# f and g of the conv attention: projected channel-major in fp32 with 32-row fp32 scores, instead of a bf16 stack built on GpSimd

## The chip, the core and the metric

The kernel runs on one core of one Trainium2 chip. The metric is the device time of one execution in microseconds (us); the smaller the better. TensorE (PE) multiplies matrices into PSUM, VectorE (DVE) and ScalarE (ACT) read PSUM and SBUF, GpSimd (POOL) works in SBUF, and SyncE (SP) issues the DMA transfers. Each engine runs its own instructions in program order, and they wait for each other on semaphores.

## The reference

Eight images (batches) of 256 tokens with 128 channels go through three blocks. The change touches the first.

```python
xf = x.reshape(b, n, c)                              # 8 x 256 x 128
f, g, hh = xf @ Wf + bf, xf @ Wg + bg, xf @ Wh + bh  # 16 columns each
attn = softmax(einsum('bnd,bmd->bnm', f, g))         # 256 x 256 scores per batch
x = gamma * (attn @ hh) @ Wv + bv + xf               # "conv" block
t = x + attention_block(ln(x))     # 8 heads of 16, softmax, W_comb, layernorm, cos, FFN of 512, layernorm
out = t + moe(ln(t))               # 32 experts, the top 2 weighted, all computed densely
```

## The kernel before

A batch of 256 tokens is two tiles (TB = 2) of 128 tokens. Each batch passes through some 28 steps: the conv block (conv_project to conv_output), the attention (attn_transpose, four attn_pair steps of two heads, two attn_context steps, attn_turn, attn_back, attn_combine), the feed-forward (ffn_transpose, two ffn_hidden, ffn_output) and the experts (moe_transpose, moe_select, moe_spread, four moe_pair steps, moe_output). The order of the steps on each engine is written out in the table ORDER: for each engine and step, eight numbers, one for each batch, and `run_steps` sorts them. So the eight batches are interleaved as a pipeline by that table, and nothing is reordered at run time.

The steps "warm_early" and "warm_late" of PE are fillers: one matmul of 128x512 zeros each (L462), whose result nobody reads. There are 71 and 33 of them, and six more at the start of the program. They stand where PE's program would otherwise wait.

In the conv block of a batch, f and g are needed with channels on the partitions, so that their product contracts over 16 channels. Before, this takes seven stages:

- PE, conv_project (L491): two fp32 matmuls of 160 columns, tokens on the partitions, give f, g (32 columns) and the value part HW (128 columns).
- DVE, conv_project (L886): adds the bias, FGs. ACT, conv_project (L719): copies HW out of PSUM after FGs is done.
- POOL, conv_project (L1154 to L1164): seven instructions split f and g into three bf16 parts each and write them as stacks of eight 16-channel pieces, FGp.
- PE, conv_stack (L503): four bf16 transposes of the stacks into PSUM; it also waits for HW, because it writes to the same bank.
- DVE, conv_stack (L892): copies them to SBUF as FGT.
- PE, conv_scores (L510): two bf16 matmuls of 256 columns over the 128 rows of the stack.
- DVE, conv_scores (L896): the negated row maximum nmx. Behind it come ACT's exponential (L726), PE's conv_turn (L518), ACT's copy ETs (L789), PE's conv_output (L526) and DVE's result T0 (named T in the rows, L908).

The result T0 opens a batch's attention: DVE takes its statistics (L831, L835), POOL the reciprocal root (var L1114, rstd L1116), DVE normalizes (L841, Y), and so on to the first attn_pair (L558), whose scores ACT turns into exponentials (EB_, L748). All conv steps of a batch use one PSUM bank: conv_ps, or the first hidden bank for batches 1 and 3. conv_project of batch b waits (semaphore s_t0) until an earlier batch has left the bank. POOL's prep_moe (L1098 to L1108) builds a constant and stands once in POOL's order.

Of the kernel before, what the change touches and what calls it, by code (L numbers as in the profile page):

```python
# [14 lines left out]
P = 128  # L15
# [27 lines left out]
        "attn_turn": (78, 95, 129, 163, 181, 208, 224, 250),  # L43
        "attn_back": (84, 102, 134, 169, 187, 213, 228, 254),
        "attn_combine": (86, 106, 138, 174, 190, 215, 230, 258),
        "ffn_transpose": (97, 133, 157, 188, 218, 238, 257, 279),
        "ffn_hidden0": (100, 136, 160, 191, 220, 240, 259, 282),
        "ffn_hidden1": (104, 139, 164, 194, 222, 242, 261, 286),
        "ffn_output": (107, 142, 168, 199, 227, 244, 263, 288),
        "moe_transpose": (123, 152, 178, 211, 234, 252, 275, 304),  # L50
        "moe_select": (130, 155, 184, 216, 236, 255, 277, 306),
        "moe_spread": (143, 167, 196, 225, 245, 266, 289, 312),
# [21 lines left out]
        "attn_back": (26, 36, 53, 83, 98, 121, 134, 155),  # L74
        "ffn_norm": (28, 41, 57, 87, 103, 124, 143, 159),
        "ffn_cos": (31, 48, 65, 94, 110, 136, 153, 167),
        "ffn_transpose": (33, 52, 74, 99, 125, 144, 158, 170),
        "ffn_hidden0": (35, 54, 76, 102, 127, 145, 161, 172),
        "ffn_hidden1": (37, 56, 78, 104, 131, 147, 162, 173),
        "moe_transpose": (46, 70, 90, 119, 139, 154, 168, 177),  # L80
        "moe_select": (50, 73, 95, 123, 141, 156, 169, 179),
        "moe_spread": (60, 81, 105, 130, 148, 163, 174, 181),
# [4 lines left out]
    },  # L87
    "vector": {
        "conv_project": (0, 2, 11, 21, 31, 57, 82, 112),
        "prep_phi": (1,),  # L90
        "conv_stack": (3, 5, 16, 27, 41, 62, 89, 118),
        "conv_scores": (4, 7, 18, 32, 47, 64, 94, 120),
# [1200 lines left out]
```

## Time and profile before

| what | value |
|---|---|
| median of 3 runs | 211.71 us (211.69 to 211.84) |
| the profiled execution's own time | 211.57 us |
| its span from first to last instruction | 209.8 us |
| PE busy | 196.0 us, 93% of the span |
| DVE, ACT, POOL busy | 131.8, 131.7, 105.7 us |
| granted TensorE clock, mean | 1.000 |

Busy time is the time in which an engine has an instruction under way. PE's 196.0 us contain the fillers, and a matmul's shown length includes the time in the pipeline, so successive matmuls overlap; what one costs PE is read from the distance of the starts. In a row of the timeline the two first numbers are start and length in us, then engine, line, operation, output, inputs and count; one fp32 matmul stands there as two records. In brackets is idle time before the row and what ended it.

### The profile page before, as it was taken

Reading aid. Unit: us, or ns where it says so; the run is one execution under the profiler, and the core shown is the slowest. Engines: PE = TensorE matmul, PEld = TensorE weight load, DVE = VectorE, ACT = ScalarE, POOL = GpSimd, SP = SyncE. Lnnn points to the kernel's source line nnn. Section 1 sums busy time; section 2 is a strip of 40 time slices with the busy share of each in tenths; the row PEclk is TensorE's granted clock in tenths of the full one; section 3 lists DMA queues with packets and bytes.
Section 4 is the critical chain, followed back from the end, with each engine's and each line's share of the span. In section 5 each row is a group of like instructions: output and inputs, shape, how many; then the busy total and the mean of one; then the engine's idle time right before and its main releaser. Section 6 shows DMA issues by size and latency. Waiting matters only on the chain. (4 is left out here: it accounts for less than half of the span.)

```text
span 209.8 us, 4691 instructions
## 1 busy us (share of the span) xinstructions
PE 196.0 (93%) x1625; PEld 141.8 (68%) x1638; DVE 131.8 (63%) x451; ACT 131.7 (63%) x256; POOL 105.7 (50%) x272
## 2 busy tenths in 40 slices
PE   7999899999989999999999999989998998999894
PEld 3655554557646877787879675867767877677683
DVE  1346776666878675986867777673663664464332
ACT  2344597988788697778689577756568427422220
POOL 4799795757475747714771534461452343311200
PEclk9999999999999999999999999999999999999999
DMA  6970000000000000000000000000000000000000
GB/s 173 354 256 0 6 0 0 5 0 3 0 0 3 2 3 0 27 3 0 5 2 25 3 0 3 25 0 3 27 0 5 0 25 2 3 25 0 30 0 25
DMA packets 6280, 5.46 MB, mean 26 GB/s; under 512 B 480, under 2 KB 5744, under 8 KB 6256
## 3 DMA queue, kind: packets, MB, share of 16 engines
q1 hardware_dynamic: 5952, 5.00, 7.5%
q8 instruction: 13, 0.21, 0.4%
q10 hardware_dynamic: 304, 0.16, 0.2%
q14 instruction: 11, 0.09, 0.1%
HBM read 4.10 MB, written 1.05 MB: 25 GB/s over the span
## 5 line engine op out<-in xcount | busy, mean ns | idle before, releaser
L748 ACT ACTIVATE EB_<-sc_ps 128x1024 f32<-128x1024 f32 x32 | 32.7, 1023 | 7.9 <-PE sc_ps L558 7.7
L657 PE MATMUL moe_ps<-val_sb,HWT 128*128 128x128 f32 x256 | 34.2, 276 | 0.7 <-DVE HWT L1057 0.7
L672 PE MATMUL hidden_ps<-XTT,keys_sb 128*128 128x256 f32 x128 | 34.3, 391 | 0.1
L1057 DVE TENSOR_TENSOR HWT<-hidden_ps,HR 128x512 f32<-128x512 f32 x32 | 22.0, 686 | 16.1 <-ACT HR L783 8.3
L657 PEld LDWEIGHTS moe_ps<-val_sb,HWT 128*128 128x128 f32 x256 | 31.0, 191 | 1.5 <-DVE HWT L1057 1.1
L783 ACT ACTIVATE HR<-hidden_ps 128x512 f32<-128x512 f32 x32 | 19.1, 597 | 14.9 <-PE hidden_ps L672 14.8
L672 PEld LDWEIGHTS hidden_ps<-XTT,keys_sb 128*128 128x128 f32 x128 | 22.0, 190 | 4.6 <-issue 2.1
L462 PE MATMUL hidden_ps<-idle_sb 128*128 128x512 bf16 x70 | 21.7, 417 | 1.8 <-DVE idle_sb L826 1.2
L558 PE MATMUL sc_ps<-HLT 32*128 32x256 f16 x256 | 19.5, 270 | 2.1 <-ACT EB_ L748 0.9
L1114 POOL TENSOR_SCALAR var<-mv 128x2 f32<-128x2 f32 x24 | 5.2, 218 | 26.7 <-DVE mv L835 25.9
L1116 POOL TENSOR_TENSOR rstd<-var,minushalf 128x2 f32<-128x2 f32 x24 | 16.8, 699 | 2.0
L558 PEld LDWEIGHTS sc_ps<-HLT 32*128 32x128 f16 x256 | 10.2, 92 | 10.2 <-issue 5.6
L570 PE MATMUL attn_ps<-EB_,PA 128*32 128x256 f32 x256 | 16.7, 384 | 0.1
L621 PE MATMUL ffn_ps<-w2T_sb,HID 128*128 128x128 f32 x128 | 15.9, 277 | 0.0
L621 PEld LDWEIGHTS ffn_ps<-w2T_sb,HID 128*128 128x128 f32 x128 | 14.9, 192 | 0.6 <-ACT HID L768 0.4
L462 PEld LDWEIGHTS hidden_ps<-idle_sb 128*128 128x128 bf16 x77 | 7.4, 105 | 7.4 <-issue 3.6
L680 PE MATMUL hidden_ps<-WT,spread 96*128 96x256 f16 x64 | 12.3, 273 | 0.0
L768 ACT ACTIVATE HID<-ffn_ps 128x512 f32<-128x512 f32 x16 | 9.6, 597 | 3.0 <-PE ffn_ps L612 2.8
L841 DVE TENSOR_SCALAR XTK<-T,mv,rstd 128x128 f32<-128x128 f32 x16 | 4.8, 343 | 9.3 <-POOL rstd L1116 9.3
L570 PEld LDWEIGHTS attn_ps<-EB_,PA 128*32 128x32 f32 x256 | 6.9, 109 | 5.3 <-ACT EB_ L748 0.7
L734 ACT ACT_TABLE_LOAD x8 | 10.3, 1283 | 0.1
L1205 POOL TENSOR_TENSOR X1B<-X,b_b 128x256 f32<-128x256 f32 x8 | 5.8, 729 | 8.4 <-DVE X L994 8.4
(179 smaller groups left out, 400.4 us busy)
## 6 DMA issues: line engine op xcount, KB each, us to landing
XT<-in_xT SPq DMA_DIRECT2D x8, 128.0 KB, 4.7
out<-OB SPq DMA_DIRECT2D x8, 128.0 KB, 1.8
X<-in_x SPq DMA_DIRECT2D x7, 128.0 KB, 4.7
keys_sb<-in_keys SPq DMA_DIRECT2D x1, 512.0 KB, 5.3
val_sb<-in_values SPq DMA_DIRECT2D x1, 512.0 KB, 6.3
pb_sb<-in_pb SPq DMA_DIRECT2D x1, 464.0 KB, 4.5
w2T_sb<-in_w2T SPq DMA_DIRECT2D x1, 256.0 KB, 4.3
pa_sb<-in_pa SPq DMA_DIRECT2D x1, 190.5 KB, 2.6
```

What stands on the lines that cost most here:

```text
L462: mm(bank[:, :], idle_sb[:, 0:P], idle_sb[:, :], start=True, stop=True)
L558: last = mm(sc_ps[i][:, t * N:(t + 1) * N], HLT[j, 0, h // 4, t * P:(t + 1) * P], HLT[j, side, h // 4, :], start=(side == 0), stop=(side = ...
L570: last = mm(attn_ps[32 * j:32 * j + 32, g * N:(g + 1) * N], PA[:, b % 2, t, h, :], EB_[:, h, t, :], start=(t == 0), stop=(t == TB - 1))
L621: last = mm(ffn_ps[:, t * C:(t + 1) * C], HID[:, k, t * P:(t + 1) * P], w2T_sb[:, k, :], start=(k == 0), stop=(k == FB - 1))
L657: last = mm(moe_ps[:, t * C:(t + 1) * C], HWT[:, k % 4, t * P:(t + 1) * P], val_sb[:, k, :], start=(k == 0 and t == 0), stop=(k == EB - 1) ...
L672: last = mm(hidden_ps[0][:, i * N:(i + 1) * N], keys_sb[:, k * EPB:(k + 1) * EPB, :].rearrange("p e h -> p (e h)"), XTT[:, b % 2, :], star ...
L680: last = mm(hidden_ps[1][:, i * N:(i + 1) * N], spread[:, 2 * q + i, :], WT[:, b % 2, :], start=True, stop=True)
L734: fn(CS[:, b % 2], ARG[:, b % 2, 2], ACT.Sin, scale=-2.0 * PI_F32).then_inc(s_y_cos, 1)
L748: fn(EB_[:, 2 * p:2 * p + 2, :, :].rearrange("p h t n -> p (h t n)"), both_ps[:, :], ACT.Exp, scale=1.0 / math.sqrt(DK)).then_inc(s_prob, 1)
L783: fn(HR[:, 2 * (q % 2):2 * (q % 2) + 2, :].rearrange("p i n -> p (i n)"), hidden_ps[0][:, :], ACT.Relu).then_inc(s_relu, 1)
L1057: V.tensor_tensor(HWT[:, half, :].rearrange("p i n -> p (i n)"), hidden_ps[1][:, :], HR[:, half, :].rearrange("p i n -> p (i n)"), ALU.mul ...
L1116: G.tensor_tensor(rstd[:, which, b, :], var[:, which, b, :], minushalf[:, :], ALU.pow).then_inc(rs, 1)
```

## The change

f and g come out of PE with channels on the partitions, in fp32. The weights of f and g lie in 64 columns (f in 0 to 15, g in 32 to 47, zeros between), and are the stationary operand; the 256 tokens of the batch are the moving one. So one matmul gives f on partitions 0 to 31 and g on 32 to 63. Two further matmuls of 128 columns give the value part. DVE adds f's bias into FT, ACT adds g's bias into GT (a new step on ACT, and the copy of HW becomes a step conv_value of its own), and two fp32 matmuls over 32 rows give the scores. The seven POOL instructions, PE's four transposes and DVE's copy of FGT of each batch are left out. The orders of all four engines are written anew: of the fillers 28 early and 19 late ones remain, and the six at the start. The transfers keep their order; the one with the weights is 382 columns instead of 381.

```diff
 ORDER = {
     "tensor": {
-        "conv_project": (0, 1, 28, 46, 68, 117, 150, 183),
-        "conv_stack": (9, 17, 41, 62, 87, 128, 161, 192),
-        "conv_scores": (12, 20, 47, 70, 103, 131, 166, 197),
+        "conv_project": (0, 3, 12, 19, 34, 83, 103, 129),
+        "conv_scores": (2, 8, 20, 30, 58, 87, 115, 141),
...
             def conv_project(b):
...
+                mm(conv_bank(b)[0:64, 0:N], wfg[:, :], XT[:, b, :], start=True, stop=True)
+                if b == 0:
                     pe.wait_ge(s_wproj_sb, 1)
                 for t in range(TB):
-                    last = mm(conv_bank(b)[:, t * (2 * D + C):(t + 1) * (2 * D + C)], XT[:, b, t * P:(t + 1) * P],
-                              wproj[:, :], start=True, stop=True)
+                    last = mm(conv_bank(b)[:, N + t * C:N + (t + 1) * C], XT[:, b, t * P:(t + 1) * P], whv[:, :],
+                              start=True, stop=True)
                 last.then_inc(s_proj_ps, 1)
 
-            def conv_stack(b):
-
+            def conv_scores(b):
+
+                pe.wait_ge(s_fT, b + 1)
+                pe.wait_ge(s_gT, b + 1)
                 pe.wait_ge(s_hW, b + 1)
-                pe.wait_ge(s_fg_l, 2 * b + 2)
...
-                    last = mm(conv_bank(b)[:, t * N:(t + 1) * N], FGT[:, b % 2, t * P:(t + 1) * P], FGT[:, b % 2, N:2 * N],
+                    last = mm(conv_bank(b)[:, t * N:(t + 1) * N], FT[:, b % 2, t * P:(t + 1) * P], GT[:, b % 2, :],
                               start=True, stop=True)
...
             def conv_project(b):
-                act.wait_ge(s_fg, b + 1)
+                act.wait_ge(s_proj_ps, b + 1)
+                if b >= 2:
+                    act.wait_ge(s_cscore_ps, b - 1)
+                fn(GT[:, b % 2, :], conv_bank(b)[32:64, 0:N], ACT.Identity, bias=bgT).then_inc(s_gT, 1)
+
+            def conv_value(b):
+                act.wait_ge(s_fT, b + 1)
                 if b >= 2:
                     act.wait_ge(s_O_ps, b - 1)
...
+                copy(HW[:, b % 2].rearrange("p t c -> p (t c)"), conv_bank(b)[:, N:2 * N]).then_inc(s_hW, 1)
...
             def conv_project(b):
                 dve.wait_ge(s_proj_ps, b + 1)
...
                 if b >= 2:
                     dve.wait_ge(s_cscore_ps, b - 1)
-                V.tensor_copy(FGT[:, b % 2, :], b16(conv_bank(b))[:, 0:2 * N]).then_inc(s_stack, 1)
+                V.tensor_scalar(FT[:, b % 2, :], conv_bank(b)[0:32, 0:N], bfT, None, ALU.add).then_inc(s_fT, 1)
...
-            def conv_project(b):
-
-
-                pool.wait_ge(s_fg, b + 1)
```

Three places show what the new table does. The first is PE right behind the two small products of the start, up to the first conv_output. Before (pa_sb holds the weights, XT the tokens, idle_sb the filler's zeros, EA the exponentials):

```order
L491 MATMUL conv_ps<-pa_sb,XT 128x160 x2
L491 MATMUL hidden_ps<-pa_sb,XT 128x160 x2
L462 MATMUL hidden_ps<-idle_sb 128x512 x7
L503 MATMUL conv_ps<-identb,FGp 128x128 x4
L462 MATMUL hidden_ps<-idle_sb 128x512 x2
L510 MATMUL conv_ps<-FGT 128x256 x2
L462 MATMUL hidden_ps<-idle_sb 128x512 x4
L503 MATMUL hidden_ps<-identb,FGp 128x128 x4
L462 MATMUL hidden_ps<-idle_sb 128x512 x2
L510 MATMUL hidden_ps<-FGT 128x256 x2
L518 MATMUL conv_ps<-ident,EA 128x128 x4
L462 MATMUL hidden_ps<-idle_sb 128x512 x3
```

The same stretch of PE in the changed program (L456 is the filler, L483 the projection of f and g, L487 the value part, L497 the scores):

```order
L483 MATMUL conv_ps<-XT,pa_sb 64x256
L487 MATMUL conv_ps<-pa_sb,XT 128x128 x2
L456 MATMUL hidden_ps<-idle_sb 128x512
L497 MATMUL conv_ps<-GT,FT 128x256 x2
L483 MATMUL hidden_ps<-XT,pa_sb 64x256
L487 MATMUL hidden_ps<-pa_sb,XT 128x128 x2
L456 MATMUL hidden_ps<-idle_sb 128x512 x3
L507 MATMUL conv_ps<-ident,EA 128x128 x4
L497 MATMUL hidden_ps<-GT,FT 128x256 x2
L515 MATMUL conv_ps<-HW,ETs 128x128 x4
L456 MATMUL hidden_ps<-idle_sb 128x512 x2
```

The scores of batch 0 now stand ahead of batch 1's projection, those of batch 1 between batch 0's conv_turn and conv_output, and the fillers up to conv_output fall from 18 to 4.

The second place is ACT at its start, up to the exponentials of batch 1. Before, and then after (L783 is the copy ETs, L720 the exponential):

```order
L708 ACT_TABLE_LOAD
L708 ACTIVATE phi_t<-phi_t 128x8
L719 COPY HW<-conv_ps 128x256
L719 COPY HW<-hidden_ps 128x256
L726 ACT_TABLE_LOAD
L726 ACTIVATE EA,den<-conv_ps,nmx 128x256 x2
L789 COPY ETs<-conv_ps 128x512
L726 ACTIVATE EA,den<-hidden_ps,nmx 128x256 x2
```

```order
L707 ACT_TABLE_LOAD
L707 ACTIVATE GT<-conv_ps,pa_sb 32x256
L713 COPY HW<-conv_ps 128x256
L720 ACTIVATE EA,den<-conv_ps,nmx 128x256 x2
L713 COPY HW<-hidden_ps 128x256
L707 ACTIVATE GT<-hidden_ps,pa_sb 32x256
L783 COPY ETs<-conv_ps 128x512
L720 ACTIVATE EA,den<-hidden_ps,nmx 128x256 x2
```

GT stands in front of HW for batch 0, and one load of an activation table is gone from this place; the whole program has 21 instead of 22.

The third place is PE near the end, from the first moe_pair of batch 6 to the third or fourth. XTT is the normalized input of the experts, WT their weights, XTK what moe_transpose (L628, after L617) turns for batch 7. Before:

```order
L672 MATMUL hidden_ps<-XTT,keys_sb 128x256 x2
L680 MATMUL hidden_ps<-WT,spread 128x256 x2
L462 MATMUL sc_ps<-idle_sb 128x512 x7
L672 MATMUL hidden_ps<-XTT,keys_sb 128x256 x2
L680 MATMUL hidden_ps<-WT,spread 128x256 x2
L657 MATMUL moe_ps<-val_sb,HWT 128x128 x4
L462 MATMUL sc_ps<-idle_sb 128x512 x5
L628 MATMUL ffn_ps<-ident,XTK 128x128 x2
L672 MATMUL hidden_ps<-XTT,keys_sb 128x256 x2
L680 MATMUL hidden_ps<-WT,spread 128x256 x2
L657 MATMUL moe_ps<-val_sb,HWT 128x128 x4
L636 MATMUL ffn_ps<-pb_sb,XTT 128x32 x2
```

The same place of PE after the change:

```order
L661 MATMUL hidden_ps<-XTT,keys_sb 128x256 x2
L669 MATMUL hidden_ps<-WT,spread 128x256 x2
L456 MATMUL sc_ps<-idle_sb 128x512 x6
L661 MATMUL hidden_ps<-XTT,keys_sb 128x256 x2
L669 MATMUL hidden_ps<-WT,spread 128x256 x2
L646 MATMUL moe_ps<-val_sb,HWT 128x128 x4
L661 MATMUL hidden_ps<-XTT,keys_sb 128x256 x2
L669 MATMUL hidden_ps<-WT,spread 128x256 x2
L646 MATMUL moe_ps<-val_sb,HWT 128x128 x4
L617 MATMUL ffn_ps<-ident,XTK 128x128 x2
L456 MATMUL sc_ps<-idle_sb 128x512
L625 MATMUL ffn_ps<-pb_sb,XTT 128x32 x2
```

The third pair of batch 6 has moved in front of batch 7's moe_transpose, into the place of five fillers, and moe_select (L636, after L625) follows the transpose with one filler between.

## Rows read from the trace of the kernel before

**Rows 1.** The page: busy us, share of the span and instructions of each engine.

```profile
PE 196.0 (93%) x1625; PEld 141.8 (68%) x1638; DVE 131.8 (63%) x451; ACT 131.7 (63%) x256; POOL 105.7 (50%) x272
```

**Rows 2.** Two of PE's waits: tile, line, releaser, total us, times, longest.

```profile
PE ffn_ps L628 <- DVE XTK L841: 2.1, 5, 0.8
...
PE sc_ps L558 <- ACT EB_ L748: 0.9, 4, 0.3
```

**Rows 3.** Windows by stage: length, busy us of each engine, granted clock, DMA share, GB/s.

```profile
0.00:25.12 25.12, 22.46 (x112) 12.85 (x115) 11.85 (x39) 10.79 (x23) 18.90 (x54) 1.00 0.51 164
25.12:157.56 132.44, 127.13 (x1205) 92.30 (x1211) 94.54 (x330) 100.53 (x195) 74.89 (x185) 1.00 0.02 6
157.56:209.80 52.24, 46.40 (x311) 36.68 (x315) 25.38 (x83) 20.36 (x40) 11.94 (x34) 1.00 0.04 11
```

**Rows 4.** The same windows, of the fillers (L462) alone: length, PE, PEld.

```profile
0.00:25.12 25.12, 13.08 (x42) 4.62 (x44) 1.00 0.51 164
25.12:157.56 132.44, 8.67 (x28) 2.82 (x33) 1.00 0.02 6
157.56:209.80 52.24, 7.30 (x27) 3.27 (x33) 1.00 0.04 11
```

**Rows 5.** Timeline of PE where no filler stands: starts give a step's cost.

```profile
102.12 0.76 PE L491 MATMUL conv_ps<-pa_sb,XT 128*128 128x160 f32 x4
102.72 0.53 PE L636 MATMUL ffn_ps<-pb_sb,XTT 128*128 128x32 f32 x4
...
107.78 0.38 PE L503 MATMUL conv_ps<-identb,FGp 128*128 128x128 bf16 x4
108.00 1.11 PE L657 MATMUL moe_ps<-val_sb,HWT 128*128 128x128 f32 x8
...
109.27 0.61 PE L558 MATMUL sc_ps<-HLT 32*128 32x256 f16 x8
109.81 0.31 PE L648 MATMUL moe_ps<-identh,WP 128*96 128x128 f16 x2
109.95 0.38 PE L510 MATMUL conv_ps<-FGT 128*128 128x256 bf16 x2
110.17 1.03 PE L672 MATMUL hidden_ps<-XTT,keys_sb 128*128 128x256 f32 x4
111.04 0.38 PE L680 MATMUL hidden_ps<-WT,spread 96*128 96x256 f16 x2
```

**Rows 6.** Timeline of PE: conv block of batch 0, and the first attn_pair.

```profile
5.17 1.41 PE L491 MATMUL conv_ps<-pa_sb,XT 128*128 128x160 f32 x4
6.37 1.27 PE L491 MATMUL hidden_ps<-pa_sb,XT 128*128 128x160 f32 x4
...
14.35 1.16 PE L526 MATMUL conv_ps<-HW,ETs 128*128 128x128 f32 x8
...
25.12 0.61 PE L558 MATMUL sc_ps<-HLT 32*128 32x256 f16 x8
```

**Rows 7.** Timeline of DVE and POOL between them.

```profile
11.22 0.69 DVE L896 TENSOR_REDUCE nmx<-conv_ps 128x2 f32<-128x512 f32 x1 [0.49 <-PE conv_ps L510]
...
20.59 0.69 DVE L961 TENSOR_TENSOR_SCAN SC<-scanmask,CS 128x256 f32<-128x256 f32 x1 [0.48 <-ACT CS L734]
20.62 1.18 POOL L1141 TENSOR_TENSOR XR<-X,rc 128x256 f32<-128x256 f32 x1
21.76 0.61 POOL L1185 TENSOR_TENSOR PA<-SC,CS 128x240 f32<-128x240 f32 x1
```

**Rows 8.** Timeline of PE and ACT near the end.

```profile
189.13 1.24 PE L462 MATMUL sc_ps<-idle_sb 128*128 128x512 bf16 x5
190.45 0.44 PE L628 MATMUL ffn_ps<-ident,XTK 128*128 128x128 f32 x2
...
190.93 0.37 ACT L772 COPY XTT<-ffn_ps 128x256 f32<-128x256 f32 x1 [2.29 <-PE ffn_ps L628]
...
192.71 0.53 PE L636 MATMUL ffn_ps<-pb_sb,XTT 128*128 128x32 f32 x4
```

More of the change, by code:

```diff
@@ L45 @@
[L45 to L52, printed above, removed]
[4 rows of a table removed]
@@ new lines @@
+        "conv_scores": (2, 8, 20, 30, 58, 87, 115, 141),
+        "conv_turn": (7, 13, 26, 44, 71, 98, 121, 157),
+        "conv_output": (9, 16, 32, 55, 74, 100, 125, 159),
+        "attn_transpose": (22, 41, 66, 90, 108, 134, 153, 177),
[7 rows of a table added]
+        "attn_turn": (45, 59, 82, 113, 131, 156, 172, 199),
+        "attn_back": (50, 63, 85, 119, 135, 161, 179, 202),
+        "attn_combine": (52, 67, 89, 122, 139, 163, 181, 206),
+        "ffn_transpose": (60, 84, 109, 137, 166, 187, 205, 224),
+        "ffn_hidden0": (62, 86, 111, 140, 170, 189, 207, 226),
@@ new lines @@
+        "ffn_hidden1": (65, 88, 114, 144, 173, 191, 209, 229),
+        "ffn_output": (69, 91, 117, 147, 176, 193, 211, 231),
+        "moe_transpose": (78, 104, 130, 160, 184, 201, 221, 242),
+        "moe_select": (81, 107, 133, 164, 186, 203, 223, 244),
+        "moe_spread": (92, 118, 148, 174, 194, 212, 232, 249),
[4 rows of a table added]
+        "moe_output": (110, 143, 171, 190, 210, 230, 246, 255),
+        "warm_early": (1, 4, 5, 6, 10, 11, 14, 15, 17, 18, 21, 23, 24, 27, 28, 37, 38, 39, 40, 47, 48, 49, 53, 61, 64, 72, 79, 80),
@@ L75 @@
[L75 to L82, printed above, removed]
[4 rows of a table removed]
+        "conv_project": (0, 4, 11, 17, 34, 55, 78, 98),
@@ L87 @@
+        "ffn_hidden0": (40, 59, 83, 109, 137, 153, 169, 180),
+        "ffn_hidden1": (42, 61, 85, 112, 139, 155, 170, 181),
+        "moe_transpose": (51, 76, 100, 127, 148, 162, 176, 186),
+        "moe_select": (54, 79, 103, 130, 151, 163, 177, 187),
+        "moe_spread": (64, 90, 116, 138, 157, 171, 182, 189),
[4 rows of a table added]
     },
     "vector": {
[L89 to L92, printed above, removed]
@@ L115 @@
-        "moe_output": (91, 119, 145, 160, 174, 186, 196, 201),
+        "prep_phi": (0,),
+        "conv_project": (1, 3, 8, 17, 28, 56, 77, 102),
+        "conv_scores": (2, 5, 16, 23, 44, 62, 87, 117),
+        "conv_turn": (4, 9, 22, 33, 49, 73, 92, 123),
+        "conv_output": (6, 12, 24, 37, 53, 74, 95, 127),
+        "proj_norm": (7, 14, 29, 39, 57, 78, 106, 128),
+        "proj_angle": (10, 19, 30, 45, 65, 84, 110, 130),
+        "proj_reduce": (11, 20, 32, 46, 70, 93, 112, 132),
+        "proj_cos": (13, 25, 38, 54, 76, 97, 116, 136),
@@ L116 @@
+        "norm_third": (50, 75, 94, 124, 146, 158, 172, 183),
+        "moe_select": (59, 83, 104, 131, 151, 161, 176, 185),
+        "moe_topk": (61, 85, 107, 135, 153, 167, 177, 187),
[4 rows of a table added]
+        "moe_output": (82, 111, 137, 152, 166, 178, 188, 193),
     },
@@ L1260, in rows, with fold @@
         return _np.broadcast_to(a, (n, a.shape[1]))
+    def fold(f, g):
+        gap = _np.zeros((f.shape[0], 32 - D), f.dtype)
+        return _np.concatenate([f, gap, g, gap], axis=1)
     x = _np.asarray(inputs["x"])
-    conv = {n: _np.asarray(inputs["L0_conv_" + n]) for n in ("Wf", "Wg", "Wh", "Wv", "bh")}
+    conv = {n: _np.asarray(inputs["L0_conv_" + n]) for n in ("Wf", "Wg", "Wh", "Wv", "bh", "bf", "bg")}
     W1, b1, W2 = (_np.asarray(inputs["L1_attn_" + n]) for n in ("W1", "b1", "W2"))
@@ L1270 @@
         "pa": _np.concatenate([
[L1271 removed]
+            _np.zeros((P, C), x.dtype), fold(conv["Wf"], conv["Wg"]), _np.pad(fold(conv["bf"][None], conv["bg"][None]).T, ((0, P - 64), (0, 0))),
+            rows("L0_conv_bv"),
             rows("L0_conv_gamma"), rows("L1_attn_phi_ffn"), W1.reshape(FB, P, NQ).transpose(1, 0, 2).reshape(P, FB * NQ),
```

147 lines of the change are left out of this document (49 added, 98 removed), and 50 rows, old and new, of the table ORDER.

## The prediction

> **What bounds the kernel now.** I read the page's engine line first: PE is busy for 196.0 of 209.8 us, the others for 106 to 132 [rows 1]. Then PE's waits: the longest, for XTK, comes to 2.1 us in total, that for ACT's exponentials EB_ to 0.9 [rows 2]. So PE's program sets the time. But it contains fillers, and a filler does nothing but stand where something is late. The windows therefore come next, cut at the first attn_pair (25.12) and at the last batch's attn_turn (157.56), once for all work [rows 3] and once for the fillers [rows 4] (97 of the 110 in the program have a record). In the first stage fillers make up 13.08 of PE's 22.46 busy us; POOL, with 18.90, is the fullest of the others. In the middle they make up 8.67 of 127.13, and PE idles for 5.3; ACT is at 100.5 of 132.4. In the last they make up 7.30 of 46.40, and PE idles for 5.8. The head is a chain of batch 0 through all engines, the middle is PE at its limit with some help from ACT, the tail again a chain. The change takes latency out of the head and puts work on PE in all of it but the tail.
>
> **The price of a step on PE.** In a stretch without fillers the distance of starts is the cost [rows 5]. The old projection (320 fp32 columns) costs 0.60 us, the four stack transposes 0.22, the old scores 0.22. For the new steps no row exists. The nearest is L672, two fp32 matmuls of 256 columns: 0.87. The new projection has 512 fp32 columns as well (256 and twice 128): between 0.87 at that rate and 0.96 at the old projection's own (0.60 x 512/320); I take 0.93, so +0.33 per batch. The new scores are twice 256 columns: 0.87, and 0.1 for going to 32 rows and back. The 0.1 comes from attn_pair, the step over 32 rows that the trace has: eight matmuls of 256 columns in 0.54 us. Two of them work on different 32-row strips at a time, so four times the 0.11 of one 256-column bf16 matmul (0.22 for L510's two) is 0.43, and 0.11 is left. The scores then cost 0.97 against 0.44 for old transposes and scores, +0.53. A gain from contracting over only 32 rows I exclude: the columns streamed are the same, and fp32 takes four times a bf16 column in L672 against L510 at any rate. Per batch +0.86, for eight +6.9 us of PE work.
>
> The Trainium skill has a rule that speaks against this step: TensorEngine Tiling (Array Packing), Key Properties, says that a change of the tiling mode drains TensorE first. The 0.11 above is all that the trace leaves room for. Without it the sum would be 0.8 us lower.
>
> **The fillers.** The program has 110, the new one 53. One costs 0.22 where PE has nothing to wait for: it has 512 bf16 columns, as the two matmuls of L510 together [rows 5]. 57 of them are 12.5 us. They are saved only where what PE waited for comes earlier or other work stands in their place; else PE idles for as long. By the old and the new program they go from 44 to 19 ahead of the first attn_pair, from 33 to 15 in the middle, from 33 to 19 behind the last attn_turn. I take the stages one by one.
>
> **Stage 1, up to the first attn_pair: -2.0 us.** From batch 0's projection to its row maximum it is now 6.05 us (5.17 to 11.22) [rows 6, 7]: POOL's seven instructions, the transposes, FGT. Afterwards: 512 columns at the early rate. This rate is half the later one: the same projection takes 1.20 us here and 0.60 at 102 us [rows 5, 6], the lower and the upper of TensorE's two levels (1.2 and 2.4 GHz), although the granted clock reads 1.00 in the whole window [rows 3]. So 1.92. Then FT on DVE and behind it HW on ACT (its queue: GT, which runs beside FT, then HW): 0.4 for the first, half of the 0.69 of a 512-column read and a little over [rows 7], 0.37 for the second, as L772 [rows 8], and some 0.3 for three handoffs. Then the scores, 0.97 at the upper level or 1.9 at the lower, I take 1.4, and 0.2 until DVE sees them: 4.6 in all, 1.45 saved (1.0 to 1.9). From the maximum to conv_output it was 3.13 us; now batch 1's scores stand between conv_turn and conv_output, in the time of the ETs copy, and I give back 0.2. Later POOL starts PA at 21.76, when its XR of batch 2 ends, although the scan was over at 21.28 [rows 7]. In the new order the XR's of batches 0 to 2 stand ahead of POOL's first norm; that frees 0.48. Sum 1.7. The other way to count, PE's program: 25 fillers less are 5.5 us, four projections and three scores more 1.32 + 1.59 = 2.9, so 2.6. I take 2.0.
>
> **Stage 2: 0.0 us.** Four projections (+1.3) and five scores (+2.65) are +4.0; 18 fillers less are -4.0 if the gaps close. What could close them: DVE loses the FGT copies and gains nothing longer, and POOL loses the splitting. ACT gains a GT of about 0.37 for each batch, 3.0 in all, and loses one of 22 table loads; in this stage it idles for 32 us [rows 3], which cover its share as long as ACT is ahead of PE. If that cover is gone, each GT delays an exponential by 0.37. New waits: DVE's FT and ACT's GT wait for the projection (and for the scores of two batches before); what is queued behind them on DVE are the statistics and norms of the batch before, on ACT the exponentials EB_, for which PE's next attn_pair waits. In the program the projection stands several steps ahead of its scores, so both waits should be over when they are reached. The bounds: +4.0 if no gap closes, and -2 if PE's idle 5.3 us shrink as well.
>
> **Stage 3: -2.5 us.** No conv work lies here, so this is order alone. One place can be worked out: batch 7's moe_transpose waits for XTK at 190.45 behind five fillers (1.1 us), and moe_select stands behind a whole pair, at 192.71 [rows 8]. XTT is there at 191.30 (190.93 + 0.37). In the new order the pair (1.98 us: 190.73 to 192.71) fills the place of the fillers, 0.9 more than they do, of which the chain to XTK hides some, and moe_select comes with the copy, 1.3 earlier. This alone is worth 1.1 or so. The 14 fillers in total are 3.1; the bounds are -1.0 and -3.5.
>
> **Sum.** -2.0 + 0.0 - 2.5 = -4.5. The profiled execution took 211.57, its span and 1.8 around it, which I leave as it is; 211.57 - 4.5 = 207.1. It lies 0.14 below the median of the runs, which is nothing here.
>
> **The rivals.** *The gaps of the middle stay gaps.* ACT is at 76% there and gets more; fillers that are taken out where ACT or DVE is late turn into waits of PE. Then +4.0 stands for stage 2: 211.1. For it speaks ACT's load [rows 3], against it that PE waited for EB_ for 0.9 us only [rows 2].
>
> *TensorE stays at its lower level for longer* (slower than before). In the head PE gets 25 fillers less and idles more. If the level changes only at about the first attn_pair, the work of the head at half speed (3 projections, 3 scores, two conv_turns and two conv_outputs on the chain: 2.8 + 2.9 + 0.9 + 1.9 = 8.5, of which I had counted 3 as slow) is 5.5 more: 212.6. It decides from a change later than about 20 us on. Against it: the fp32 matmuls are long, and fill much of what the fillers filled. The Trainium skill, TensorE: Matmul & The Clock Gate, on the HAM clock gate, says that the low clock is the default and activity releases it, which is this rival's mechanism; the slow start in the rows agrees.
>
> *The 32-row scores or the 64-column projection cost much more than the rows around them* (a switch of 0.3 in place of 0.1 on both): 16 x 0.2 = 3.2, so 210.3.
>
> *The latency saved in the head isn't what sets the start of the middle*: stage 1 gives 0, 209.1.
>
> **Chances.** The forecast, with its terms anywhere between their bounds, 0.60; a late level 0.12; open gaps 0.14; dear steps 0.07; no gain in the head 0.07. The forecast alone lies between 204 and 209.5; with the open gaps, and none of the late level but its near end, the range is 203.6 to 211.3. A difference under 0.2% (0.4 us) can't be told from none. The open gaps reach from 209.5 to 212.5: half faster, 0.04 of the 0.14 within the bound, 0.03 slower; of the dear steps 0.01 falls on slower. So faster 0.60 + 0.07 + 0.06 + 0.07 = 0.80, same 0.04, slower 0.16.
>
> **What would show it.** Right: the first row maximum at 9 to 10 us, the first attn_pair at 23, fillers' busy time below half of before, PE idle at no more than 15 us in all, a projection at 0.93 and scores at 0.97 between starts, moe_select of batch 7 right behind XTT. Wrong: PE waits for EB_, FT or GT above 3 us in total; 0.43 instead of 0.22 between fillers beyond 12 us; scores above 1.2. If the middle stage is longer by 3 us or more, its term is the one that failed.

## The result, and the profile of the changed kernel

The change makes the kernel slower: 213.49 us in the median of 15 executions against 211.71 for the kernel before, a ratio of 1.0069 with a 95% interval of 1.0043 to 1.0095. The ratio, here and below, leaves out the executions that are more than 1.5% longer than the fastest of their kernel; medians, ranges and counts take in all. The forecast of 207.1 was wrong, and so was its side. The times also scatter: 212.0 to 215.2 us, where the kernel before stays within 210.8 and 212.1.

The profiled execution took 213.17 us. Its page, with the engine line and the line of the granted clock (a digit for each of 40 slices of 5.3 us):

```profile
PE 193.4 (92%) x1571; PEld 141.3 (67%) x1581; DVE 132.8 (63%) x443; ACT 134.0 (63%) x263; POOL 88.5 (42%) x216
...
PEclk9999987999999999999999999999999999999999
```

PE is busy for 2.6 us less than in [rows 1], and yet the span is 211.1 in place of 209.8: PE idles 17.7 us, before 13.8. The windows, cut where the first attn_pair (25.48) and the last attn_turn (159.16) start, once for all work and once for the fillers (L456) alone:

```profile
0.00:25.48 25.48, 22.15 (x91) 12.42 (x93) 12.38 (x40) 11.38 (x27) 13.56 (x32) 1.00 0.51 162
25.48:159.16 133.68, 127.06 (x1184) 93.31 (x1190) 95.06 (x320) 103.65 (x200) 64.01 (x155) 0.99 0.02 6
159.16:211.10 51.94, 44.21 (x299) 35.62 (x301) 25.41 (x83) 18.97 (x38) 10.94 (x30) 1.00 0.04 11
```

```profile
0.00:25.48 25.48, 7.28 (x18) 2.18 (x19) 1.00 0.51 162
25.48:159.16 133.68, 3.13 (x10) 1.30 (x15) 0.99 0.02 6
159.16:211.10 51.94, 4.05 (x15) 1.85 (x19) 1.00 0.04 11
```

| stage | forecast | measured | missed by |
|---|---|---|---|
| 1, to the first attn_pair | -2.0 | +0.36 (25.48 for 25.12) | 2.4 |
| 2, to the last attn_turn | 0.0 | +1.24 (133.68 for 132.44) | 1.2 |
| 3, behind it | -2.5 | -0.30 (51.94 for 52.24) | 2.2 |
| around the span | 0 | +0.3 (2.07 for 1.77) | 0.3 |

The four misses add up to the 6.1 us between 207.1 and 213.17.

**Where stages 1 and 2 lost it.** PE's timeline (start, length, tile and inputs, number of records, and in brackets the idle time before and what ended it):

```profile
4.99 1.11 PE L483 MATMUL conv_ps<-XT,pa_sb 128*64 128x256 f32 x2
6.04 1.22 PE L487 MATMUL conv_ps<-pa_sb,XT 128*128 128x128 f32 x4
7.05 0.63 PE L456 MATMUL hidden_ps<-idle_sb 128*128 128x512 bf16 x1
8.32 2.04 PE L497 MATMUL conv_ps<-GT,FT 32*128 32x256 f32 x4 [0.63 <-ACT HW L713]
10.29 1.11 PE L483 MATMUL hidden_ps<-XT,pa_sb 128*64 128x256 f32 x2
...
12.35 1.35 PE L456 MATMUL hidden_ps<-idle_sb 128*128 128x512 bf16 x3
13.54 0.60 PE L507 MATMUL conv_ps<-ident,EA 128*128 128x128 f32 x4
14.07 1.12 PE L497 MATMUL hidden_ps<-GT,FT 32*128 32x256 f32 x4
15.13 1.16 PE L515 MATMUL conv_ps<-HW,ETs 128*128 128x128 f32 x8
...
17.08 0.62 PE L483 MATMUL conv_ps<-XT,pa_sb 128*64 128x256 f32 x2 [0.36 <-DVE T L897]
...
18.18 0.60 PE L507 MATMUL hidden_ps<-ident,EA 128*128 128x128 f32 x4
...
25.48 0.61 PE L547 MATMUL sc_ps<-HLT 32*128 32x256 f16 x8 [0.51 <-DVE HLT L963]
...
29.88 1.53 PE L515 MATMUL conv_ps<-HW,ETs 128*128 128x128 f32 x8
31.34 1.94 PE L559 MATMUL attn_ps<-EB_,PA 128*32 128x256 f32 x16
33.20 0.98 PE L483 MATMUL conv_ps<-XT,pa_sb 128*64 128x256 f32 x2
34.12 0.71 PE L487 MATMUL conv_ps<-pa_sb,XT 128*128 128x128 f32 x4
```

Two things are to be seen. First, steps have half the rate up to about 13.5 us: a projection takes 2.06 (4.99 to 7.05, and 10.29 to 12.35) where at 17.08 it takes 1.10 (to 18.18), and the scores of batch 0 take 1.97 where those of batch 1, at 14.07, take 1.06. In the kernel before, the rate rose within the seven fillers that run from 7.44 to 9.88. (The granted clock reads 1.00 in this window of either kernel, as it did in [rows 3]; the lower level is read from the steps. In the profile of e6, below, the granted clock shows such a stretch too.) Second, between 30 and 35 us TensorE falls back for a while, and this the granted clock does show, with the 7 of the PEclk line: L515 goes from 1.0 to 1.46 (29.88 to 31.34), L559 takes 1.86 (31.34 to 33.20) and the 64-column matmul 0.92 (33.20 to 34.12) for 0.55. PE doesn't wait while it lasts (28.24 to 35.7); in the 5 us from 25 to 30 it was busy for 3.99, in the kernel before for 4.61. That doesn't settle the cause: in the profile of e7, below, PE does the same steps from 25.17 to 30.17, is busy for 3.99 as well, and does not fall back behind them.

The first row maximum, on DVE, did come earlier, but less than forecast (11.22 in [rows 7]):

```profile
7.30 0.47 DVE L881 TENSOR_SCALAR FT<-conv_ps,pa_sb 32x256 f32<-32x256 f32 x1
...
10.40 0.69 DVE L885 TENSOR_REDUCE nmx<-conv_ps 128x2 f32<-128x512 f32 x1 [2.63 <-PE conv_ps L497]
```

and conv_turn and conv_output behind it stand in PE's program behind batch 1's projection and scores, so that conv_output starts at 15.13, later than the 14.35 of [rows 6]. The exponentials that conv_turn needs are there at 12.06, but PE is at batch 1's projection until 12.35 and at three fillers until 13.54.

**Where stage 3 lost it.** DVE near the end, before:

```profile
187.27 0.68 DVE L1057 TENSOR_TENSOR HWT<-hidden_ps,HR 128x512 f32<-128x512 f32 x1
...
189.79 0.60 DVE L841 TENSOR_SCALAR XTK<-T,mv,rstd 128x128 f32<-128x128 f32 x2 [1.17 <-POOL rstd L1116]
```

DVE and PE there after the change:

```profile
188.64 0.68 DVE L1046 TENSOR_TENSOR HWT<-hidden_ps,HR 128x512 f32<-128x512 f32 x1
189.88 0.69 DVE L1046 TENSOR_TENSOR HWT<-hidden_ps,HR 128x512 f32<-128x512 f32 x1 [0.56 <-PE hidden_ps L669]
190.49 0.48 DVE L825 BATCH_NORM_STATS2 st<-T 128x6 f32<-128x128 f32 x2
...
192.42 0.60 DVE L835 TENSOR_SCALAR XTK<-T,mv,rstd 128x128 f32<-128x128 f32 x2 [1.17 <-POOL rstd L1105]
...
193.08 0.44 PE L617 MATMUL ffn_ps<-ident,XTK 128*128 128x128 f32 x2 [0.43 <-DVE XTK L835]
...
193.98 0.63 PE L625 MATMUL ffn_ps<-pb_sb,XTT 128*128 128x32 f32 x4 [0.46 <-ACT XTT L766]
```

The new table puts the whole of norm_third of batch 7 behind two pairs of batch 6 on DVE (HWT), where it stood behind one. The second pair waits 0.56 us for PE. So the statistics start at 190.49 and the transpose at 193.08, 2.63 later than in [rows 8]. 1.60 of this was there when the stage began, 1.03 is new. Then moe_select follows 0.90 behind the transpose in place of 2.26, and 1.36 come back. What is left of the stage's gain is 0.3.

### The profile page after: what moved, and what is told of

Its sections match the earlier page's. It is cut to its first block and busy times, and to the rows that moved or that the text cites. A ratio compares the mean times of both kernels' runs of the same rounds, so it can differ in the third digit from the quotient of the medians.

```text
span 211.1 us, 4523 instructions
## 1 busy us (share of the span) xinstructions
PE 193.4 (92%) x1571; PEld 141.3 (67%) x1581; DVE 132.8 (63%) x443; ACT 134.0 (63%) x263; POOL 88.5 (42%) x216
## 5 line engine op out<-in xcount | busy, mean ns | idle before, releaser
L1103 POOL TENSOR_SCALAR var<-mv 128x2 f32<-128x2 f32 x24 | 4.6, 192 | 35.5 <-DVE mv L829 34.9
L559 PE MATMUL attn_ps<-EB_,PA 128*32 128x256 f32 x256 | 17.0, 399 | 0.1
L456 PE MATMUL hidden_ps<-idle_sb 128*128 128x512 bf16 x28 | 10.4, 465 | 1.6 <-DVE idle_sb L820 1.2
L559 PEld LDWEIGHTS attn_ps<-EB_,PA 128*32 128x32 f32 x256 | 7.4, 112 | 6.1 <-issue 1.3
L669 PEld LDWEIGHTS hidden_ps<-WT,spread 96*128 96x128 f16 x64 | 5.9, 98 | 5.8 <-DVE HWT L1046 1.6
L801 ACT COPY WT<-moe_ps 96x256 f16<-96x256 f16 x8 | 2.9, 364 | 10.0 <-PE moe_ps L637 10.0
L1163 POOL TENSOR_SCALAR var<-zsq 128x2 f32<-128x2 f32 x8 | 2.1, 260 | 16.5 <-ACT ZQ L788 16.5
```

Of the source, the lines that this page charges most:

```text
L456: mm(bank[:, :], idle_sb[:, 0:P], idle_sb[:, :], start=True, stop=True)
L559: last = mm(attn_ps[32 * j:32 * j + 32, g * N:(g + 1) * N], PA[:, b % 2, t, h, :], EB_[:, h, t, :], start=(t == 0), stop=(t == TB - 1))
L669: last = mm(hidden_ps[1][:, i * N:(i + 1) * N], spread[:, 2 * q + i, :], WT[:, b % 2, :], start=True, stop=True)
```

## The experiments

Three theories. A: TensorE's level. The new program lets it rise later and fall back. B: the price. The 64-column and 32-row steps take more of PE than the forecast gave them. C: order. The table loses in the tail what it should have won. Each kernel below was timed beside the kernel before on the same chip; that kernel's median there was 211.4 to 211.8.

**Both new matmuls widened (e1).** f and g's weights padded with zeros to 128 columns, FT and GT to 128 rows of zeros; the weights' load is longer by 64 columns.

```diff
-                mm(conv_bank(b)[0:64, 0:N], wfg[:, :], XT[:, b, :], start=True, stop=True)
+                mm(conv_bank(b)[:, 0:N], wfg[:, :], XT[:, b, :], start=True, stop=True)
...
-        FT = sb("FT", [32, 2, N])
-        GT = sb("GT", [32, 2, N])
+        FT = sb("FT", [P, 2, N])
+        GT = sb("GT", [P, 2, N])
```

> The changed kernel, with the weights of f and g padded by zeros to 128 columns and FT and GT to 128 rows of zeros, so that PE streams the same columns and never goes to 64 columns or 32 rows in the conv steps (the weight transfer is 64 columns longer). Theory A, the upper level of TensorE's clock comes later and falls back because the narrow matmuls and fewer fillers work the array less: the level rises near 10 us instead of 13.5 and doesn't fall back at 30; 210.5 us. Theory B, the level is left alone and only the switches go: projection from 1.10 to 0.9 and scores from 1.06 to 0.9 between starts, about 0.35 for each batch, of which the dense middle gives some 1.5 back: 212. Theory C, the order of the tail and the fillers' gaps decide: 213.3, as the changed kernel.

Measured: 211.51, ratio 0.9998 (0.9976 to 1.0019), 2.0 under the changed kernel. A projection takes 0.95 (20.46 to 21.41) for 1.10, scores 0.87 for 1.06. The rate rises at about 12 us, the first attn_pair starts at 24.41, and nothing falls back at 30 us. The time lies between A's 210.5 and B's 212: the padding makes the steps cheaper and the rate rises sooner, so this run can't tell the two apart.

**Seven fillers put back (e2)**, two of them ahead of the scores of batch 0, one ahead of its conv_turn, four around its second and third attn_pair.

```diff
-        "warm_early": (1, 4, 5, 6, 10, 11, 14, 15, 17, 18, 21, 23, 24, 27, 28, 37, ...
+        "warm_early": (1, 1.1, 1.2, 4, 5, 6, 6.1, 10, 11, 14, 15, 17, 18, 21, 23, 24, 27, 28, 28.1, 28.2, 29.5, 31.5, 37, ...
```

> The changed kernel with seven more fillers, at places of the head where PE waited: two ahead of the scores of batch 0, one behind its projection of batch 1, four around the first attn_pairs. Theory A: the level rises 2 to 3 us earlier and doesn't fall back at 30 us, 211 us, and the runs lie closer together. Theory B or C: 213.5 or a little more (up to 1.5 us, seven fillers).

Measured: 211.39, but with a scatter from 209.4 to 215.8; ratio 0.9965 (0.9935 to 0.9994). It is near A's 211, but the executions don't lie closer together, as A had it, and fillers alone don't settle it: in the profiled execution the rate rose only at about 16 us (first attn_pair 27.06); no fall-back followed, and the middle took 132.20.

**The kernel before with 25 fillers fewer ahead of its first attn_pair (e3)**: 13 are left there, as in the new table, and the six of the start.

```diff
-        "warm_early": (2, 3, 4, 5, 6, 7, 8, 10, 11, 13, 14, 15, 16, 18, 19, 22, 23, 24, 27, 29, 30, 31, 32, 33, 35, 36, 37, 38, 39, 40, 42, 43, 44, 45, 48, 50, 51, 52, ...
+        "warm_early": (2, 3, 10, 15, 18, 27, 29, 30, 31, 35, 36, 48, 50, ...
```

> The kernel before, with 25 of the 38 fillers ahead of the first attn_pair taken out, as many as the change takes out there; nothing else is touched. Theory A: the level rises later than 9.5 us, the head gets longer, 212.5 to 214 us, with a spread of runs like that of the changed kernel. Theory B or C: fillers stand only where PE waits, 211.7 us, the spread as before.

Measured: 212.9, ratio 1.0066 (1.004 to 1.0092): the same loss as the change's, without any new matmul. In the profiled execution the rate rises at about 13 us, and the first attn_pair starts at 25.98, 0.86 later than with the fillers. In the windows of 5 us, the clock is lowered from 20 to 30 us; in the first five PE stands still for 2.25:

```profile
20.00:25.00 5.00, 2.75 (x20) 2.17 (x20) 2.84 (x7) 2.42 (x4) 3.77 (x10) 0.82 0.02 5
25.00:30.00 5.00, 4.32 (x36) 2.50 (x39) 4.49 (x19) 3.67 (x9) 4.23 (x16) 0.84 0.01 2
```

So these fillers weren't idle cover: without them the rate rose later and fell back in this execution. This is A by another road, a fall-back after PE stood still.

**The new steps in the order of before (e4)**, with all 110 fillers.

```diff
 ORDER = {
     "tensor": {
-        "conv_project": (0, 3, 12, 19, 34, 83, 103, 129),
-        "conv_scores": (2, 8, 20, 30, 58, 87, 115, 141),
+        "conv_project": (0, 1, 28, 46, 68, 117, 150, 183),
+        "conv_scores": (12, 20, 47, 70, 103, 131, 166, 197),
...
```

> The new conv steps in the order of before: the table of before without the stack, the splitting and the stack's copy, with HW's copy right behind GT, and with all 110 fillers. Theory A: level as before, up at 9.5 us; the head is 1 to 2 us shorter, the middle longer by PE's extra work, 212 to 214. Theory B: the extra work of PE (1.1 us a batch) stays on the path of PE in the middle and in part in the head, 214 to 217. Theory C (the new order is the loss): below the changed kernel, 211 to 212.

Measured: 221.16, ratio 1.0454 (1.0424 to 1.0484), more than any of the three theories had. The first attn_pair starts at 28.88, the middle takes 137.75, the tail is that of before. So the new steps cost 3.8 us ahead of the middle and 5.3 in it unless the order makes room for them; the new table earns 7.7 us (221.16 against 213.49), and its middle is as good as forecast.

**The paddings one by one (e5, e6).**

```diff
-        wfg = pa_sb[:, A_WFG:A_WFG + 2 * 32]
+        wfg = pa_sb[:, A_WFG:A_WFG + 128]
...
```

> Only the f and g projection is padded to 128 stationary columns; the scores stay with 32 rows. With both padded the kernel measured 211.5 us and the rate of TensorE rose at about 12 us and did not fall back. Theory A1 (the 64-column projection is what delays the rise and leads to the fall-back): first attention pair at about 24.4 to 24.8 us, no slice of lower clock behind 15 us, 211.5 to 212.0 us. Theory A2 (it is the 32-row scores): the rate rises at about 13.5 us as in the changed kernel, clock lower around 30 us, 213 to 213.5 us. In either case a projection should take about 0.95 us and the scores about 1.06 us.

Measured with the projection padded alone: 212.11, ratio 1.0021 (0.9992 to 1.005), spans from 209.1 to 211.5. Rate up at about 13 us, first attn_pair 25.11, no fall-back at 30 us in the profile.

```diff
-        FT = sb("FT", [32, 2, N])
...
+        FT = sb("FT", [P, 2, N])
...
```

> Only the scores are padded to 128 rows (FT and GT with 96 rows of zeros); the projection keeps its 64 columns. Theory A2 (the 32-row scores are what delays the rise of the rate): rise at about 12 us, no lower clock around 30 us, 211.5 to 212.0 us. Theory A1 (the projection): 213 to 213.5 us with the fall-back. Scores about 0.87 us in place of 1.06, projection about 1.10.

Measured with the scores padded alone: 212.25, ratio 1.0014 (0.9999 to 1.003), spans from 209.1 to 209.9 only. Rate up at about 14 us, first attn_pair 25.21. But that is its second rise in this execution. PE's rows and the page's line of the granted clock (the second and third digits stand for 5.2 to 15.7 us):

```profile
4.57 0.65 PE L484 MATMUL conv_ps<-XT,pa_sb 128*64 128x256 f32 x2
...
5.69 0.38 PE L457 MATMUL hidden_ps<-idle_sb 128*128 128x512 bf16 x1
7.96 2.05 PE L500 MATMUL conv_ps<-GT,FT 128*128 128x256 f32 x4 [1.89 <-ACT HW L716]
...
PEclk9769999999999999999999999999999999999999
```

The projection of batch 0 takes 1.12 (4.57 to 5.69), so the level was up by then. PE then waits 1.89 us ahead of the scores, and in this wait the granted clock falls to 0.50 and stays there until about 14, with steps of twice the length. The profile of e7, below, shows the same after a wait of 1.64 us. So in some executions it is the wait ahead of the scores of batch 0 behind which TensorE is slow, and not a late first rise.

Neither theory of the pair is right by itself: of the 2.0 us that both paddings bring in the median, that of the projection alone brings 1.4 and that of the scores alone 1.2, but only that of the scores takes the long executions away.

**The statistics of norm_third as a step of their own (e7)**, for batch 7 ahead of pair 1 of batch 6; nothing else moves.

```diff
+        "norm_third_stats": (49.5, 74.5, 93.5, 123.5, 145.5, 157.5, 171.5, 181.5),
         "norm_third": (50, 75, 94, 124, 146, 158, 172, 183),
```

> The changed kernel with the statistics of norm_third of batch 7 ahead of pair 1 of batch 6 in VectorE's order (its application stays where it is). Theory C (in the tail the gain was lost because these statistics stand behind a pair that waits for TensorE): the XTK of batch 7 is ready 1.2 us sooner, the router transpose of batch 7 then waits for TensorE's pair 2 and starts about 0.6 us sooner, spread of batch 7 about 39.0 us behind the last attention turn's batch in place of 39.6: 212.9 us. If theory C is wrong (the tail is bounded by TensorE or by the expert pairs): 213.5 us. The head is the same program as in the changed kernel, so its profile also shows whether the fall-back around 30 us returns.

Measured: 211.9, ratio 1.001 (0.9986 to 1.0035). From the last attn_turn to the last moe_spread 38.99 (157.81 to 196.80) for 39.63 in the changed kernel, -0.64 as C had it. The other 1.0 of the gain in the median (1.6) lies in two things that the edit was not aimed at: the level (up at the first projection, down from about 7.6 to 14.4 us as in e6's profile, and no fall-back at 30 us; fewer long spans) and the time around the span (below).

**Both (e8).**

```diff
...
+        FT = sb("FT", [P, 2, N])
...
+        "norm_third_stats": (49.5, 74.5, 93.5, 123.5, 145.5, 157.5, 171.5, 181.5),
```

> Both paddings and the statistics of norm_third moved. Theories A and C together: 211.5 for the paddings less 0.6 for the tail, 210.9 us, under both kernels. If only A holds: 211.5 us.

Measured: 210.25, ratio 0.9924 (0.9908 to 0.9941), under both kernels. Its rows on DVE and PE:

```profile
189.02 0.60 DVE L842 TENSOR_SCALAR XTK<-T,mv,rstd 128x128 f32<-128x128 f32 x2 [0.59 <-POOL rstd L1114]
...
190.33 0.38 PE L621 MATMUL ffn_ps<-ident,XTK 128*128 128x128 f32 x2
```

XTK is done 0.7 before its transpose now; the transpose no longer waits for it but stands behind pair 2. So behind this wait PE's own order is the next bound.

**The changed kernel once more (e9)**, without an edit.

> The changed kernel as it is, a second time. If the wide scatter of its times (212.0 to 215.2 us, spans 209.8 to 213.4) and the time around the span (1.8 to 3.1 us, before 1.8) belong to the program, both return here: median 213 to 214, some spans of 211 and more. If they came from that chip or that hour: median near 212, time around the span 1.8.

Measured: 215.12 in the median of four (211.7 to 216.4), spans from 209.8 to 213.5, ratio 1.0104 (1.0004 to 1.0204). The same program again, and its profile differs from the first one:

```profile
14.62 2.07 PE L497 MATMUL hidden_ps<-GT,FT 32*128 32x256 f32 x4
16.62 2.08 PE L515 MATMUL conv_ps<-HW,ETs 128*128 128x128 f32 x8
18.49 1.03 PE L456 MATMUL hidden_ps<-idle_sb 128*128 128x512 bf16 x2
19.49 0.62 PE L483 MATMUL conv_ps<-XT,pa_sb 128*64 128x256 f32 x2
...
27.89 0.61 PE L547 MATMUL sc_ps<-HLT 32*128 32x256 f16 x8 [0.51 <-DVE HLT L963]
```

Here the rate rises only at about 19 us, the first attn_pair starts at 27.89, and a fall-back from about 33 us comes on top (middle 133.67); the span is 213.5. So the scatter belongs to the program, and between these two profiles it is the time at which the level rises: of the 2.4 us between the spans 2.41 lie ahead of the first attn_pair.

**Paddings, statistics and two or four fillers ahead of the scores of batch 0 (e10, e11).** B here means that these fillers don't move the rise.

```diff
-        "warm_early": (1, 4, 5, ...
+        "warm_early": (1, 1.1, 1.2, 4, 5, ...
```

> Both paddings, the moved statistics (that combination measured 210.25 us, first attention pair at 24.44, the rate of TensorE up at about 13 us) and two more fillers in the 0.63 us in which TensorE waits ahead of the scores of batch 0. Theory A (the stage up to the first attention pair is set by when the rate rises): the rate rises at 10 to 12 us, first attention pair at about 23.5 us, 209.3 us. Theory B (the rate's rise is not moved by fillers there): scores of batch 0 start 0.3 us later, 210.4 us.

Measured with two: 208.99, ratio 0.9904 (0.9869 to 0.9938), the four spans within 207.1 to 207.4. The head on PE:

```profile
4.99 1.22 PE L485 MATMUL conv_ps<-XT,pa_sb 128*128 128x256 f32 x2
6.00 1.06 PE L489 MATMUL conv_ps<-pa_sb,XT 128*128 128x128 f32 x4
6.86 1.49 PE L458 MATMUL hidden_ps<-idle_sb 128*128 128x512 bf16 x3
8.13 1.50 PE L501 MATMUL conv_ps<-GT,FT 128*128 128x256 f32 x4
9.47 0.59 PE L485 MATMUL hidden_ps<-XT,pa_sb 128*128 128x256 f32 x2
...
23.29 0.61 PE L551 MATMUL sc_ps<-HLT 32*128 32x256 f16 x8 [0.35 <-DVE HLT L970]
```

The rate rises within the scores of batch 0, at about 9 us, and the first attn_pair starts at 23.29.

> As the run with two more fillers, with four. The fillers end about 0.9 us behind the time at which the scores could start. Theory A: the rate is up when the scores of batch 0 run (1.0 us in place of 2.0), which gives back the 0.9 us and more in the projection of batch 1: 209.0 to 209.5 us. Theory B: 0.9 us lost, 211.0 us.

Measured with four: 209.44, ratio 0.9934 (0.99 to 0.9968). The scores start 0.86 later and take 1.33 as with two; the first attn_pair starts at 24.14, later by the same 0.85. The number lies where A had put it, but not by its mechanism: with the level still lower when they start, the scores did not shrink to 1.0, and in this execution the two extra fillers only delay. (The shortest span with four is 207.1, as with two.)

**The fillers without the paddings (e12).** A1 and A2 have another meaning here than in e5 and e6; the expectation states it.

```diff
-        "warm_early": (1, 4, 5, ...
+        "warm_early": (1, 1.1, 1.2, 4, 5, ...
...
+        "norm_third_stats": (49.5, 74.5, 93.5, 123.5, 145.5, 157.5, 171.5, 181.5),
```

> The moved statistics and the two fillers ahead of the scores of batch 0, without the paddings: the fourth corner of the square (neither 211.90, paddings 210.25, both 208.99). Theory A1 (a matmul over 32 rows or 64 columns, long as it is, does not bring or hold TensorE's upper level as a full one does): the level rises later than with the paddings in some executions and falls back in some, so the spans scatter from 207 to over 211, median 210 to 211.5 us. Theory A2 (only time in which TensorE stands still counts against the level): the fillers do as much without the paddings as with them, first attention pair at about 23.7 us, spans within 1 us, median 209.3 us.

Measured: 211.42, from 208.5 to 216.3, ratio 0.994 (0.991 to 0.9969), spans from 206.7 to 214.5. The profiled execution, with a span of 213.0, on PE:

```profile
4.99 1.11 PE L484 MATMUL conv_ps<-XT,pa_sb 128*64 128x256 f32 x2
...
7.05 1.49 PE L457 MATMUL hidden_ps<-idle_sb 128*128 128x512 bf16 x3
8.47 2.07 PE L498 MATMUL conv_ps<-GT,FT 32*128 32x256 f32 x4
...
14.80 2.07 PE L498 MATMUL hidden_ps<-GT,FT 32*128 32x256 f32 x4
16.80 2.08 PE L516 MATMUL conv_ps<-HW,ETs 128*128 128x128 f32 x8
...
21.72 1.06 PE L508 MATMUL hidden_ps<-ident,EA 128*128 128x128 f32 x4
22.58 0.68 PE L457 MATMUL hidden_ps<-idle_sb 128*128 128x512 bf16 x2
```

PE does not idle once between 4.99 and 23 us, and works at half rate all the way to about 22.6. Against e10 nothing is different but the zeros that make the two matmuls full (and the six memsets that write them), and there the rate rises at 9. This is one of e12's long executions, and e10 and e12 have one profile each; the shortest span of e12, 206.7, lies under all four of e10. So without the padding the rate can rise late although PE doesn't wait; it doesn't always. The median and the scatter are those of A1; A2, which had all spans within 1 us, is out.

The stages of the profiled executions side by side (starts of the first attn_pair, the last attn_turn, the last moe_spread, in us; the rise is read from the first steps at full rate; each row is one execution, and those of e2, e9 and e12 are long ones of their kernel):

| kernel | rate up at | attn_pair | middle | turn to spread | span |
|---|---|---|---|---|---|
| before | 7.4 to 9.9 | 25.12 | 132.44 | 39.86 | 209.8 |
| changed | 13.5 | 25.48 | 133.68 | 39.63 | 211.1 |
| changed, e9 | 19 | 27.89 | 133.67 | 39.61 | 213.5 |
| e1, both padded | 12 | 24.41 | 132.49 | 39.62 | 208.9 |
| e2, seven fillers | 16 | 27.06 | 132.20 | 39.62 | 211.2 |
| e3, before with 25 fewer | 13 | 25.98 | 132.29 | 39.86 | 210.5 |
| e4, new steps, old order | 9 | 28.88 | 137.75 | 39.84 | 218.8 |
| e5, projection padded | 13 | 25.11 | 132.00 | 39.62 | 209.1 |
| e6, scores padded | by 4.6, again 14 | 25.21 | 132.68 | 39.62 | 209.9 |
| e7, statistics | by 4.6, again 14 | 25.65 | 132.16 | 38.99 | 209.2 |
| e8, padded, statistics | 13 | 24.44 | 132.56 | 38.98 | 208.3 |
| e10, e8 and two fillers | 9 | 23.29 | 132.49 | 38.97 | 207.1 |
| e11, e8 and four fillers | 10 | 24.14 | 132.50 | 38.97 | 208.0 |
| e12, e7 and two fillers | 22.6 | 29.49 | 132.14 | 38.99 | 213.0 |

And all executions: of the six kernels whose scores have 32 rows in the new order (the changed one twice, e2, e5, e7, e12) 27 of 68 executions have a span of 211 us or more; of the five with padded scores (e1, e6, e8, e10, e11) none of 44, and of the kernel before, beside them, none of 83. That holds for the long executions only. Lowered stretches are not gone with the padding: the granted clock of the whole execution is 0.992 or less in 3 of the 12 of e1 and in 4 of the 12 of e6. And the fall-back at about 30 us, which both profiles of the changed kernel have, is missing in e2, e5, e7 and e12 too, whose scores have 32 rows; what brings it stays open.

## Why the prediction was wrong

**The price of a step: the right kind, a little low.** Projection 1.10 for the forecast 0.93, scores 1.06 for 0.97, so +1.12 per batch for +0.86. Padded to 128 they take 0.95 and 0.87, so 0.15 and 0.19 of it are due to the narrow shape; the 0.1 that attn_pair had shown is a half to two thirds of that. TensorEngine Tiling (Array Packing), Key Properties, of the Trainium skill had said that a change of the mode drains TensorE, and the runs agree in the direction and give the size. But B explains little of the time: with the dear steps and without them the middle of the new order takes 132.0 to 132.7 wherever nothing falls back. The rival of the dear steps is out.

**Stage 2, 0.0: right where the level holds.** There the middle is within -0.4 and +0.25 of the 132.44 before. The open gaps, which would have given +4.0, didn't come: fillers fell from 8.67 to 3.13 busy us as the work rose. The +1.24 measured is the fall-back: L515, L559 and L483 take 0.4, 0.9 and 0.4 more than later on. The step that failed here is that the sum had no term for a lower level in the middle; that the gaps close came true.

**Stage 1, -2.0: the mechanism was right, its condition was not.** In the forecast's own terms: the row maximum came 0.82 earlier for 1.45, from there to conv_output it took 1.60 more for 0.2, and behind it 0.42 less for 0.48 (POOL's PA now starts when the scan ends). The forecast took the scores of batch 0 half at the upper level (1.4 us) and everything behind them at it. With the level up at 9 us, e10 has scores of 1.34 and its first attn_pair at 23.29, -1.83. The changed kernel runs them, the projection of batch 1 and three fillers at half rate, and what the order had won (nmx 0.8 earlier) is gone at conv_output. The step that failed is the sentence against the second rival, that "the fp32 matmuls are long, and fill much of what the fillers filled". They filled the time, and that was not enough to bring the level: in the profile of e12 PE is busy for 18 us without it. That rival is what came in. But the point from which I let it decide, 20 us, was too late: 13.5 us is enough to take all of stage 1's gain, since the projections ahead are on the chain, and I had no fall-back in it at all.

The Trainium skill, TensorE: Matmul & The Clock Gate, Part 1: The HAM clock gate, says that the gate is set by how busy PE has been lately and does not start with the kernel, so that the same kernel is released at different points. The two profiles of the changed program, 13.5 and 19 us, agree with the second half. On the first half they leave a question: in their profiles e12 and e10 are equally busy up to 9 us, and only in the one with padded matmuls does the rate rise there. By the second half one pair of executions can differ by itself; that padding the scores has a part in it rests on the counts above, 27 long ones among 68 executions against none among 44.

**Stage 3, -2.5: wrong.** I worked out PE's side, the pair in the place of five fillers and moe_select right behind the copy, and that came (0.90 for 2.26). I left DVE's order out: the table had also moved norm_third behind the second pair there, and "of which the chain to XTK hides some" was in truth the chain to XTK getting 1.26 longer: from the first HWT (188.64) to XTK 3.78 us, in the kernel before 2.52 (187.27 to 189.79). Moving the statistics alone gives 0.64 back (e7), as C had it; with them stage 3 is -0.9 in e10. The rest of the -2.5 was taken from the number of fillers, and did not come: they are busy for 3.25 us less, but PE idles for 7.7 us of the stage in place of 5.8.

**Around the span, 0: open.** It was 1.75 to 1.88 us in every execution of the kernel before, and 1.8 to 3.2 in the changed one (median 2.5), in e1, e2, e5, e6 and again in e9. In e3, e4 and e10 it was 1.8 throughout, in e7, e8 and e12 mostly, and in e11 in half of the executions, with single ones up to 3.6. About 0.7 of the 1.78 us between the medians are this. The profile shows nothing outside the span, and the only edit between the changed kernel and e7 is the step of the statistics; why that should matter isn't known, and no run was made for it. It is a part of the miss of 6.1 that stays without a cause.

## What to carry to other kernels

A filler isn't only a stand-in for a wait: before fillers go, look at what else keeps TensorE busy while its level may rise or fall, and check the rate of its first steps as well as the granted clock. The steps with few rows or columns took longer here than full ones (scores 1.06 against 0.87), and with 32-row scores the long executions came; padding with zeros to 128 by 128 took 0.15 to 0.19 us off each step, and with two fillers at the right place and the statistics as a step of their own turned a loss of 0.7% into a gain of 1%. When a step is moved on one engine, follow the same step on every other engine: the gain of the tail was worked out on PE and lost in VectorE's list.

## What was not expected of the hardware

- TensorE stayed at half rate for 18 us of unbroken work in one execution (e12, with 32-row and 64-column fp32 matmuls); in one of the same program padded (e10) it left it at 9 us.
- It fell back to the lower level at about 30 us in the changed kernel, after 5 us in which it was busy for 3.99, and in e3 between 20 and 25 us, of which it was busy for 2.75. In e7 it did not, after the same steps and the same 3.99.
- In e6 and e7 it was at the upper level by 4.6 us, fell to 0.50 in a wait of 1.89 and 1.64 us and came back at about 14, where other executions show no early rise.
- The same program differed by 2.4 us in the start of its first attn_pair between two executions (25.48 and 27.89).
- A matmul padded from 64 to 128 columns or from 32 to 128 rows took less time per step, not more.
